# Attention stage: up products into the score ring, down product in halves, two projections as partition exchanges

## What is computed

```python
xn = layernorm(x); gate, clock, p = xn@gate_w, xn@clock_w, xn@p_w
q, k, v = xn@Wq, xn@Wk, xn@Wv             # 16 heads of 8
q, k = rope(l2norm(q)), rope(l2norm(k))   # scaled by running sums of softplus(gate), of softplus(clock)*exp(p)
o = softmax(q k^T, causal) @ v            # x1 = xn-side residual + o@out_w
x2 = x1 + gelu(layernorm(x1)@mlp_w1) @ mlp_w2    # 128 -> 512 -> 128
```

## Time and profile before

| | |
|---|---|
| median of three runs | 2212.62 us |
| the profiled execution | span 2164.4 us from first to last instruction; its time outside the span is not listed |
| TensorE busy | 1849.2 us (85%), 12576 matmul records |
| weight loads | 954.5 us (44%), beside TensorE |
| VectorE busy | 1703.8 us (79%) |
| ScalarE busy | 1474.7 us (68%) |
| GpSimd busy | 1165.1 us (54%) |
| attention stage | from the start to about 770 us |
| granted TensorE clock, whole span | 0.931 of full speed |

### The profile page before, as it was taken

How to read it: one execution, slowest core, us unless ns; L and a number is a source line. 1 busy time by engine, 2 the same in 40 slices (tenths; PEclk the granted TensorE clock), 3 DMA queues, 4 the chain that set the end, 5 groups by cost and what they waited for, 6 DMA issues and landing times. The chain is left out here.

```text
span 2164.4 us, 37241 instructions
## 1 busy us (share of the span) xinstructions
PE 1849.2 (85%) x12576; PEld 954.5 (44%) x12600; DVE 1703.8 (79%) x3547; ACT 1474.7 (68%) x2917; POOL 1165.1 (54%) x720
## 2 busy tenths in 40 slices
PE   6999999999998459957889889898898988659996
PEld 2566666656665259952222222222222222124453
DVE  7778868877863437854899999999999998976776
ACT  5888888888885138845656666666666666437775
POOL 2122232242221027871789999999999998840001
PEclk9999999999999669977899999999999998879998
DMA  4100010011001012221100111001111100023333
GB/s 169 36 26 26 28 49 26 26 36 41 21 25 33 20 50 77 88 72 42 30 25 27 34 35 34 27 30 30 31 35 35 35 31 30 21 67 90 97 84 78
DMA packets 103708, 97.35 MB, mean 45 GB/s; under 512 B 9137, under 2 KB 86113, under 8 KB 103137
## 3 DMA queue, kind: packets, MB, share of 16 engines
q1 hardware_dynamic: 95584, 75.34, 12.4%
q0 software_dynamic: 6784, 18.10, 2.5%
q10 hardware_dynamic: 1152, 1.54, 0.2%
HBM read 45.87 MB, written 28.10 MB: 34 GB/s over the span
## 5 line engine op out<-in xcount | busy, mean ns | idle before, releaser
L1935 POOL TENSOR_TENSOR hc<-h,c_rep 128x1024 f32<-128x1024 f32 x256 | 627.8, 2463 | 137.9 <-DVE h L1899 136.7
L1899 DVE TENSOR_TENSOR_SCAN h<-decay,bank 128x1024 f32<-128x1024 f32 x241 | 551.0, 2286 | 22.5 <-issue 0.9
L1757 ACT ACTIVATE decay<-bank,neg_a_r 128x510 f32<-128x510 f32 x512 | 322.6, 683 | 257.5 <-PE bank L1634 257.1
L1618 PE MATMUL bank<-u_in,sel_rows 32*128 32x512 f32 x964 | 287.9, 675 | 95.7 <-DVE h L1899 95.6
L1634 PE MATMUL bank<-delta,sel_rows 32*128 32x512 f32 x1024 | 338.8, 677 | 0.9 <-ACT decay L1757 0.9
L1886 DVE TENSOR_TENSOR bank<-bank,b_rep 128x1024 f32<-128x1024 f32 x241 | 291.2, 1208 | 34.8 <-PE bank L1618 33.0
L992 POOL DMA_INDIRECT rows_in_dram<-row,idx x64 | 63.3, 989 | 318.3 <-DVE row L965 303.7
L574 ACT ACTIVATE es<-bank 128x384 f32<-128x384 f32 x512 | 208.9, 499 | 22.1 <-PE bank L373 21.8
L1618 PEld LDWEIGHTS bank<-u_in,sel_rows 32*128 32x128 f32 x964 | 76.0, 191 | 276.7 <-DVE h L1899 199.7
L1649 PE MATMUL bank<-hc,y_sel 128*32 128x512 f32 x1024 | 149.6, 660 | 0.8 <-POOL hc L1935 0.8
L1656 PE MATMUL bank<-xpad,w_conv 128*128 128x512 f32 x256 | 133.0, 634 | 3.2 <-ACT xc L1819 1.6
(11 more groups left out here) (341 smaller groups left out, 4170.0 us busy)
## 6 DMA issues: line engine op xcount, KB each, us to landing
r_tw<-r_o_t SPq DMA_DIRECT2D x96, 128.0 KB, 2.3
xvs<-xv SPq DMA_DIRECT2D x16, 512.0 KB, 2.9
u_wide<-u_rep_dram SPq DMA_DIRECT2D x30, 256.0 KB, 3.5
xs<-rows_in_dram SPq DMA_DIRECT2D x72, 68.0 KB, 1.8
front<-in_x_dram SPq DMA_DIRECT2D x16, 256.0 KB, 2.9
w<-in_w_dram SPq DMA_DIRECT2D x2, 2048.0 KB
xlb_dram<-front SPq DMA_DIRECT2D x16, 256.0 KB, 2.3
xlb_m<-xlb_dram SPq DMA_DIRECT2D x16, 256.0 KB
```

Of the source, the lines that this page charges most:

```text
L1618: last = pe.matmul(BD[n % 2][:, i * STEP:(i + 1) * STEP], sel[at:at + 32, r, :], u_in[p if n < NS else q][at:at + 32, hf, :], start=True, ...
L1757: act.activation(decay[n % 4][:, i, :, 1:], seq(DL[i])[:, :, 1:], ACT.Exp, scale=c["neg_a_r"][:, hf, g:g + 1]).then_inc(s["n_da"], 1)
L1899: dve.tensor_tensor_scan(flat(h[n % RING]), decay[n % 4].rearrange("p i b t -> p (i b t)"), flat(drive_0) if by_pool else BD[n % 2], 0.0, ...
L1935: pool.tensor_tensor(hc[n % RING][:, :, :], h[n % RING][:, :, :], c_rep[p if n < NS else q][:, :].unsqueeze(1).to_broadcast([P, 2, STEP]), ...
```

## The change

1. The four up products go into the four RING banks, one behind the other, ahead of the clock projection; they wait for exps 5, and quad 6 waits for the last gelu. The four gelus stand together behind av_copy 2.
2. The down product is issued in two halves: the first before quad 7, the second behind weigh 6. The residual add waits for both.
3. `w_qs` and `w_ks` are no longer loaded or projected. VectorE multiplies q (then k) by the sine into `rot_b`, SyncE exchanges neighbouring partitions into `rot_s` by two DMAs, and VectorE subtracts `rot_s`.
4. TensorE's order: ssq ahead of quad 0; weigh 7 behind quad 0; back 3 behind quad 1; quad 2 and weigh 1 ahead of the transposes of `xl2`; affinities behind ssk; weigh 2 and quad 4 ahead of the ranks. ScalarE: av_copy 3 behind exps 0, exps 2 ahead of av_copy 0, o_t behind both. VectorE: expert choice behind heads_o 0; rotation products of q ahead of the residual add.
5. GpSimd's L985 waits for the centring of `xl2`.

```diff
+        def swap(sp, sem):
+            for to in range(2):
+                sp.dma_start(rot_s[to:P:2, :], rot_b[1 - to:P:2, :]).then_inc(sem, 16)
 # sp_step, front
+                sp.wait_ge(s["f_rb"], one_on)
+                swap(sp, s["f_qsw"])
+                sp.wait_ge(s["f_kb"], one_on)
+                sp.wait_ge(s["f_rq"], one_on)
+                swap(sp, s["f_ksw"])
                 sp.wait_ge(s["f_xlb"], one_on)
 # pe_step
             def up(n):
-                pe.matmul(M[:, :], c["w_up"][:, n * P:(n + 1) * P], h_t[:, :], ...
+                pe.matmul(RING[n], c["w_up"][:, n * P:(n + 1) * P], h_t[:, :], ...
             if tail:
                 pe.wait_ge(s["m_ht_sb"], k - 2)
-                up(0)
+                pe.wait_ge(s["s_exp"], 8 * (k - 2) + 6 if late else 8 * PAIRS)
+                for n in range(FC):
+                    up(n)
             if late:
+                if tail:
+                    pe.wait_ge(s["m_gelu"], 4 * k - 8)
                 quad(6, k - 2, p)
...
             if tail:
                 pe.wait_ge(s["m_gelu"], 4 * k - 8)
-                for j in range(TS): ...
+                down(range(0, 2))
             if late:
                 quad(7, k - 2, p)
-            if front:
-                pe.wait_ge(s["f_pe"], k + 1)
-                project(FB, c["w_qs"], s["f_qs"])
-            if late:
                 weigh(6, k - 2, p)
-                weigh(7, k - 2, p)
+            if tail:
+                down(range(2, TS))
+            if front:
+                (ssq)
             if scores:
                 quad(0, k - 1, q)
             if late:
-                back(3, k - 2)
-            (ssq)
+                weigh(7, k - 2, p)
...
             if scores:
                 quad(1, k - 1, q)
-            if front:
-                pe.wait_ge(s["f_mq"], k + 1)
-                project(FA, c["w_ks"], s["f_ks"])
+            if late:
+                back(3, k - 2)
             if scores:
                 weigh(0, k - 1, q)
+                quad(2, k - 1, q)
+                weigh(1, k - 1, q)
             if tail:
                 transposes(M, xl2, s["m_x2t"])
 # dve_step
+                dve.tensor_tensor(seq(rot_b), seq(FA), sin, ALU.mult).then_inc(s["f_rb"], 1)
 (residual add, x2)
-                dve.tensor_tensor(seq(rot_b), seq(FB), sin, ALU.mult).then_inc(s["f_rb"], 1)
...
+                dve.wait_ge(s["f_qsw"], 32 * k + 32)
+                dve.tensor_tensor(rot[:, :], rot[:, :], rot_s[:, :], ALU.subtract).then_inc(s["f_rq"], 1)
 # pool_step, front
                 pool.wait_ge(s["f_back"], k + 1)
+                if tail:
+                    pool.wait_ge(s["m_xl2"], k - 2)
                 pool.tensor_tensor(mag[:, 1, :], mag[:, 1, :], one_up[:, :], ALU.subtract)
```

More of the change, by code:

```diff
@@ L275, in attention @@
         end = sb("end", [1, E])
-        of = sb("of", [1, ETILES])
-        before = sb("before", [1, ETILES])
+        of, before = (log[0:1, 0, n * ETILES:(n + 1) * ETILES] for n in range(2))
         hi = sb("p_hi", [E * FC, P], bf16)
@@ L417, in up, with down @@
             def up(n):
-                pe.matmul(M[:, :], c["w_up"][:, n * P:(n + 1) * P], h_t[:, :], start=True, stop=True).then_inc(s["m_up"], 1)
+                pe.matmul(RING[n], c["w_up"][:, n * P:(n + 1) * P], h_t[:, :], start=True, stop=True).then_inc(s["m_up"], 1)
+            def down(tiles):
+                for j in tiles:
+                    for n in range(FC):
+                        last = pe.matmul(M[:, j * P:(j + 1) * P], g[:, n, j * P:(j + 1) * P], w_down[:, n, :],
+                                         start=n == 0, stop=n == FC - 1)
+                last.then_inc(s["m_dn"], 1)
             if late:
@@ L457, in pe_step @@
                 pe.wait_ge(s["m_gelu"], 4 * k - 8)
[L458 to L462, removed]
+                down(range(0, 2))
             if late:
                 quad(7, k - 2, p)
+                weigh(6, k - 2, p)
+            if tail:
+                down(range(2, TS))
             if front:
[L466 to L470 removed]
+                pe.wait_ge(s["f_sq"], k + 1)
+                pe.wait_ge(s["f_rb"], k + 1)
+                pe.matmul(FA[:, :], c["ones_blk"], square[:, :], start=True, stop=True).then_inc(s["f_ssq"], 1)
             if k == 1:
@@ L500, in pe_step @@
                 transposes(M, xl2, s["m_x2t"])
[L501 to L508, removed]
             if scores:
@@ L516, in pe_step @@
             if front:
-                pe.wait_ge(s["f_ka"], k + 1)
+                pe.wait_ge(s["f_kb"], k + 1)
                 pe.wait_ge(s["f_sk"], k + 1)
                 pe.matmul(FB[:, :], c["ones_blk"], square[:, :], start=True, stop=True).then_inc(s["f_ssk"], 1)
+            if tail:
+                pe.wait_ge(s["m_x2t_sb"], k - 2)
+                for j in range(TS):
+                    last = pe.matmul(M[:, j * E:(j + 1) * E], o_t[:, j * P:(j + 1) * P], c["cent"][:, :], start=True, stop=True)
+                last.then_inc(s["m_aff"], 1)
             if scores:
@@ L528, in pe_step @@
                 transposes(M, o_tok[p], s["m_ot"])
+            if scores:
+                weigh(2, k - 1, q)
+                quad(4, k - 1, q)
             if tail:
@@ L541, in pe_step @@
                 last.then_inc(s["r_rank"], 1)
-            if scores:
-                weigh(2, k - 1, q)
-                quad(4, k - 1, q)
             if mid:
@@ L593, in act_step @@
                 act.activation(v_a[q][:, :, :, 0:DH], FA.rearrange("p (j h d) -> p j h d", j=TS, h=H), ACT.Copy).then_inc(s["f_vaug"], 1)
-            if tail:
-                since(act, s["m_dn"], k - 3)
-                gelu(0)
             if late:
@@ L599, in act_step @@
             if tail:
-                gelu(1)
+                since(act, s["m_dn"], 2 * k - 6)
+                for n in range(FC):
+                    gelu(n)
             if front:
@@ L647, in act_step @@
                 exps(0, k - 1)
+            if late:
+                av_copy(3, k - 2)
             if tail:
@@ L680, in act_step @@
             if scores:
+                exps(2, k - 1)
                 av_copy(0, k - 1)
-                exps(2, k - 1)
+            if tail:
+                act.wait_ge(s["m_x2t"], k - 2)
+                act.activation(o_t[:, :], M[:, :], ACT.Copy).then_inc(s["m_x2t_sb"], 1)
             if front:
@@ L822, in dve_step @@
                 centred(h_tok, x2, mv_m, rs_m, s["m_yn"])
-            if front:
-                dve.wait_ge(s["f_ra"], k + 1)
-                dve.wait_ge(s["f_rb"], k + 1)
-                dve.tensor_tensor(rot[:, :], rot[:, :], rot_b[:, :], ALU.add).then_inc(s["f_rq"], 1)
             if tail:
```

111 lines of the change are left out of this document (48 added, 63 removed).

## The result

The changed kernel takes 2282.12 us (median of 4), the kernel before on the same chip 2212.77 (4 runs): ratio 1.0319, 95% interval 1.0305 to 1.0334. It is 69 us slower; forecast were 50 us slower, 2262.6 in a range of 2215 to 2287. The forecast's narrower own range, 2245 to 2282, is missed by 0.1 us.

What follows compares the result with a forecast made beforehand. TensorE was taken to set the pace (busy 39.89 of 41.83 us), ScalarE 5.8 us behind your written order; +52 for 13 passes, +2 start, -4 end gave +50: 2212.6 to 2262.6 us, range 2215 to 2287.

Steps and rivals of the forecast that it cites:

- TensorE stays the bound and is relieved: Rival: quads 1 and 2 find their exps done, pass 40.0 us, 2185 us in all; chance 0.16.
- half a chain: Rival: ScalarE catches up by quad 2, only +0.5 to +1.5 us per pass, about 2225 us; chance 0.12.
- slow exchanges: Rival: each DMA exchange lands 4 us later than assumed, +2 us more per pass, 2290 us; chance 0.04.
- Halves: Down product in two halves of 1.88 us: residual add starts at 17.4 instead of 16.07, 1.4 us later.
- Back 3: Back 3 behind quad 1: ln3 at 26.0, ScalarE idle 1.9 us; quad 1 to quad 2 +0.4 us.
- Quad 2 to quad 3: Weigh 1 and `xl2` transposes come in, back 0 waits for ScalarE: 6.0 us for 3.56, +2.4, before contention.
- contention: GpSimd's stall moves from the centring of `xl` to VectorE's scan and clip: quad 3 later by +1.1 us.
- Start: Steps 0 to 2, without tail: VectorE waits uncovered for the exchange in step 0, +2 us (0 to +5).
- End: Steps 16 to 18: ups and gelus of step 18 -4.7 us, steps 16 and 17 +0.7; -4 (-7 to 0).
- The 48.2 us outside the span: Median 2212.6 against span 2164.4: 48.2 us taken to lie outside the span, carried over unchanged.
- 13 passes: Full passes of the attention loop, steps 3 to 15: 4.0 us more each, 45.8 us per pass, +52 us.

Runs made afterwards that it cites:

- e10: The changed kernel without GpSimd's wait for the centring of `xl`: 2254.54 us, ratio 1.0433 to the kernel before.
- e3: The changed kernel with the down product whole again, ahead of quad 7: 2212.83 us, ratio 1.0235 to the kernel before.
- e2: The changed kernel with back 3 again ahead of quad 1, its copy on ScalarE moved with it: 2188.59 us, ratio 1.0124 to the kernel before.
- e6: The kernel before with the partition exchange alone, in place of the two projections: 2220.30 us, ratio 1.0065.
- e11: The kernel before with the ups back to back and GpSimd's wait for the centring of `xl`, nothing else: 2131.95 us, ratio 0.9868.
- e5: The changed kernel, unedited, profiled again on another chip: 2278.03 us, ratio 1.0331 to the kernel before.
- e1: The kernel before, unedited, for a second profile: 2164.11 us.
- e4: The changed kernel with back 3 ahead of quad 1 and the down product whole: 2172.85 us, ratio 1.0062 to the kernel before.
- e7: The kernel before with the ups alone changed: four in a row, gelus together, quad 6 waiting for the last gelu: 2188.23 us, ratio 0.9910.
- e8: The changed kernel with back 3 ahead of quad 1, ssk ahead of back 0 and ScalarE's norm and log instructions reordered, halves kept: 2229.52 us, ratio 1.0104.

## Why the prediction held, and where it was off

The table gives the times into the pass: the kernel before, the forecast, `e10` (A, no remote wait) and the changed kernel less 1.45 us (its h_t starts at 3.78; at 2.31 in `e10`, at 2.36 before). In the kernel before quad 6 doesn't wait for the gelus.

| | before | forecast | e10 | changed - 1.45 |
|---|---|---|---|---|
| quad 6 | 5.08 | 8.05 | 8.10 | 8.14 |
| residual add | 16.07 | 17.4 | 18.00 | 18.03 |
| ln of the second norm | 18.6 | 19.5 | 20.05 | 20.08 |
| quad 1 | 23.60 | 23.66 | 24.19 | 24.21 |
| ln3 | 23.03 | 26.0 | 26.52 | 26.55 |
| quad 2 | 29.14 | 29.63 | 30.16 | 30.18 |
| quad 3 | 32.70 | 36.7 | 38.28 | 37.16 |
| end of the pass | 41.83 | 45.8 | 47.65 | 46.54 |

*The mechanism is right.* ScalarE's written order decides. The halves delay the residual add, ln stands ahead of all exps, and the exps ahead of TensorE's quads; `e3` takes exactly this wait away. Back 3 behind quad 1 delays ln3 by the forecast size, and `e2` takes that wait away. TensorE's relief buys nothing, in `e6` even alone. The rival "TensorE stays the bound and is relieved" falls with the 3.76 us ahead of ln, "half a chain" with quad 3 at 37.2, "slow exchanges" with 0.2 us of waiting in the whole execution (0.3 in `e6`).

*Halves: mis-sized by 0.6 us a pass.* The step "first half 11.55 to 13.4, quad 7 to 14.75, weigh 6 to 15.4, second half to 17.3" gave 1.88 to a half and nothing to the gaps. Each half does take 1.88, and quad 7 starts at 13.49, as forecast. But weigh 6 starts 0.33 later than forecast and takes 0.79 instead of 0.64, and the add starts 0.27 behind the second half instead of 0.1. The distances from the add to quad 3 are the forecast's within 0.1, so 0.6 a pass, 8 us in all, are this term. A part of it is contention that the forecast didn't look for: the centring of `front`, 1.12 us before, runs beside GpSimd's L979 and L982 now, and `heads_o` for weigh 6 stands behind it.

```profile
512.52 2.69 DVE L766 TENSOR_SCALAR front<-front,f_mean_var,f_rstd 128x128 f32<-128x128 f32 x4
```

*Back 3.* The forecast put +0.4 on quad 1 to quad 2: measured 5.97 for 5.54, as computed. But undoing it brings 2.5 us (5.97 to 3.46). Both are right: the new order takes the `xl` wait, its transposes and weigh 1 out of that stretch and puts them behind quad 2, and back 3 spends what this would have saved. The split of the forecast, 0.4 for back 3 and 3.5 behind quad 2, is therefore no price list: from quad 1 to quad 3 the sum came out (3.9 forecast, 3.85 measured), but 2.9 of it go with back 3 alone (`e2`). A difference to before is not the price of an edit in the new order.

*Quad 2 to quad 3*: forecast +2.4 and +1.1 for contention, 7.1 us; measured 6.98. The stall was moved and not removed in all three orders (`xl` 3.27, or clip 1.31, or clip 0.87). The Trainium skill (GPSIMD Engine Reference, Specifications) says that GpSimd contends with VectorE where that reads two SBUF inputs or works in a 2-port mode. The traces agree that the two get in each other's way, on either side: the scan, which reads two SBUF inputs, is not slowed (1.21 to 1.23 in all orders), but GpSimd's L986, which starts 0.24 us behind it, takes 2.05 instead of 1.27. What the rule can't say is the price: the changed kernel, with the wait, is 1.1 us a pass better than `e10`, and 1.1 us were earned in `e11`. The forecast named only the loss at the clip. What `xl` done 2 us sooner brings to the scan was already in its 2.4, which took the clip to be done at 30.8; so the sum came out right.

*Start: mis-sized.* Forecast +2 (0 to +5). The first h_t of the loop, in step 3, comes at 113.8 to 117.3 us in the three profiles of the changed kernel and at 101.5 to 101.9 in the three of the kernel before: +12 to +15. The exchange is not it (0.2 us). The waits of TensorE in the first 60 us, and from 60 to 115 us (in total, times, longest):

```profile
PE bank L481 <- DVE rot_b L812: 6.2, 2, 3.2
PE bank L521 <- DVE rot_b L866: 3.5, 1, 3.5
...
PE bank L411 <- ACT avs L587: 5.5, 2, 4.2
```

In the bare steps TensorE waits for `rot_b` ahead of each norm sum, since the bank of the projection is free only after both rotation products. One bank now has both readers, where two banks had one each; before, TensorE waited 0.2 and 0.6 us at these two sums in step 0. Step 1 then runs at a granted clock of 0.66 in this profile and 0.89 in `e5` (45 to 60 us), where the kernel before had 1.00. In step 2 back 3 behind quad 1 holds VectorE's queue, ScalarE waits 3.37 us for the clip, and TensorE 4.25 at back 0; that wait is gone in `e2`, but the start is still 10.5 us longer there. In `e6`, with the exchange alone, it is 2.4 us longer, so most of the loss comes from the new order, which has less to cover it in a step without tail. The runs don't price its parts.

*End: mis-sized the other way.* Forecast -4 (-7 to 0). From h_t of step 16 to ScalarE's table load for the experts it takes 123.6 to 125.4 us instead of 130.5 to 132.3: -5 to -9. The ups and gelus of the last step gain 5.8 us where 4.7 were forecast, and the down product behind them takes 3.84 instead of 5.86, at a granted clock of 1.00 instead of 0.63.

```profile
833.14 3.84 PE L436 MATMUL bank<-w_a,g 128*128 128x128 f32 x32 [0.78 <-ACT g L591]
```

*The 48.2 us outside the span*: wrong, they were a difference between two kinds of chip. It did not hurt the forecast, since it was carried unchanged and only the difference counted; that is luck, and it holds only as far as the two kernels lose the same on B. (The 32.37 us of VectorE in the prediction are 32.38 in the earlier trace rows, which changes nothing.)

*The sum.* 69 us measured, 50 forecast.

| | forecast | runs |
|---|---|---|
| start to step 3 | +2 | +12 to +15 |
| 13 passes | +52 | +66 to +70 without the remote waits |
| steps 16 to 18 | -4 | -5 to -9 |
| together | +50 | +71 to +76; by the medians +69 to +74 |

The passes are 543.7 us before and 623.4 to 626.5 in the changed kernel, with remote waits of 13.0 to 13.8 us at h_t in them. Of the 14 to 18 us beyond the forecast, 9 are 0.7 more a pass (0.6 from the halves, the rest behind quad 3), and the others lie in the passes at a lower clock. The clock was no term of the forecast, which took the 1.00 of the earlier trace rows to stay: TensorE's idle time has a price behind it as well. So each term but the end was too small, the start most of all for its size, and the end hid a part of that. That the remote wait costs the kernel before as much per pass as the changed one, and so drops out, follows only from times (15 to 20 us of 46), not from a profile: this stays argued.

## What to carry to other kernels

In a written order the worth of an edit is not read from the busiest engine: TensorE was relieved by 1.7 us a pass, and the pass grew by about 4.7, since the queues of ScalarE and VectorE held something late ahead of something urgent. Ask of each moved piece what stands behind it on its reader's queue (ln ahead of all exps). Try the parts alone before the whole: two of them together (`e11`) give -1.3%, all of them +3.2%. And before a span is compared with a median, see that both are from the same kind of chip.

## What was not expected of the hardware

- Two kinds of chip, 2.1% apart with the same program (2160 and 2206 us), at the same granted clock (0.93). The difference shows as waits with no releaser on the core: 1.3 us at `h_t`, the first instruction of ScalarE's step, in ten of the passes, and 3.7 us at the activation `hid` of the experts' loop. What they are is open.
- On A eight tiles of the experts' loop take 17.7 us (`e1`), on B 22.8 (the changed kernel, once the waits have set in).
- TensorE's clock fell to 1.2 GHz for 3.6 us behind an idle time of 2.36 us that had followed two of 1.75 and 0.83. The changed kernel, `e3` and `e10`, which all have this wait of 2.36 us, had passes of 0.86 to 0.96, up to 4.7 us longer; before, `e2`, `e4`, `e7` and `e11` kept 1.00 up to 600 us. The sum of the idle time alone doesn't tell them apart: `e2` is idle 5.6 us a pass (43.95 - 38.35) at 1.00, `e3` 4.65 (44.50 - 39.85) at 0.96. `e2`'s longest wait is 1.5 us. `e6` and `e8`, with longest waits of 1.7 and 1.8, had single passes of 0.93 and 0.96.
